# Toeplitz blocks of the later steps: tiles of 8 channel pairs, two in turn, in place of tiles of 4 pairs, four in turn

## The reference

```
y = x + depthwise_causal_conv1d(x, taps) + conv_bias     # 128 taps, of which 64 can reach a time step
h = taps (as the initial state, batch 128)
for t in 0..63:                                          # GRU
    r, z = sigmoid(y[:, t] @ W_i{r,z} + h @ W_h{r,z} + b)
    n    = tanh(y[:, t] @ W_in + b_in + r * (h @ W_hn + b_hn))
    h    = (1 - z) * n + z * h
    out[:, t] = y[:, t] + h
```

## Time and profile before

| | |
|---|---|
| median of 3 runs | 1245.08 us (1244.24 to 1248.44) |
| the profiled execution | 1242.02 us, of it the span of the trace 1240.2 us |
| PE, PEld, DVE, ACT busy | 96%, 80%, 43%, 40% of the span |
| DMA | 98.0 MB, mean 79 GB/s |
| Toeplitz tile loads | 128 of 128 KB, median 3.4 us from issue to landing |
| x unit loads | 64 of 256 KB, median 4.8 us |

### The profile page before, as it was taken

The page is one execution under the profiler, slowest core; times in us unless marked ns, Lnnn a source line. Parts: engine busy times, 40 slices in busy tenths (PEclk is TensorE's granted clock), DMA queues, the critical chain, the costliest instruction groups (busy, mean ns, idle before and its releaser), DMA issues.

```text
span 1240.2 us, 14912 instructions
## 1 busy us (share of the span) xinstructions
PE 1184.8 (96%) x5516; PEld 991.3 (80%) x5516; DVE 539.4 (43%) x807; ACT 493.2 (40%) x929; POOL 19.5 (2%) x19
## 2 busy tenths in 40 slices
PE   1599999999999999999999999999999999999997
PEld 0597788888878888888888888888888888888886
DVE  2254667666656333333333333333333333333333
ACT  1235677767765333323333323333322333332332
POOL 1040000000000000000000000000000000000000
PEclk9999999999999999999999999999999999999999
DMA  9999888888862211110011111011111001111100
GB/s 140 208 253 172 177 185 194 185 175 188 183 166 74 62 35 34 34 34 26 25 34 34 34 34 34 22 29 34 34 34 34 25 25 34 34 34 34 34 14 21
DMA packets 298482, 98.00 MB, mean 79 GB/s; under 512 B 226976, under 2 KB 292512, under 8 KB 296400
## 3 DMA queue, kind: packets, MB, share of 16 engines
q1 hardware_dynamic: 295920, 96.80, 35.5%
q10 hardware_dynamic: 2528, 0.76, 0.5%
HBM read 63.38 MB, written 34.14 MB: 79 GB/s over the span
## 4 chain that ended last, share of the span: by engine, by line
PE 90%; SPq 5%; ACT 2%; DVE 1%; issue 1%; DMA 1%; ACTq 0%; DVEq 0%
PE bank L737 81%; PE bank L759 4%; PE bank L726 3%; SPq L286 3%; PE bank L705 2%; SPq L331 1%; SPq L294 1%; ACT x_parts L522 1%; ACT tmp L532 0%; SPq L342 0%; DVE x_parts L632 0%; ACT bank L492 0%; DMA xT<-xres 0%; DMA toep_span<-tap_pad 0%; SPq L318 0%
## 5 line engine op out<-in xcount | busy, mean ns | idle before, releaser
L737 PE MATMUL bank<-w_ih_hi,xT_hi 128*128 128x512 f32 x768 | 306.7, 399 | 0.0
L737 PE MATMUL bank<-w_ih_hi,xT_lo 128*128 128x512 f32 x768 | 301.0, 392 | 0.0
L737 PE MATMUL bank<-w_ih_lo,xT_hi 128*128 128x512 f32 x768 | 300.9, 392 | 0.0
L737 PE MATMUL bank<-w_hh_hi,hT_hi 128*128 128x512 f32 x768 | 299.8, 390 | 0.0
L737 PE MATMUL bank<-w_hh_lo,hT_hi 128*128 128x512 f32 x768 | 299.7, 390 | 0.0
L737 PE MATMUL bank<-w_hh_hi,hT_lo 128*128 128x512 f32 x768 | 298.8, 389 | 0.0
L737 PEld LDWEIGHTS bank<-w_ih_hi,xT_lo 128*128 128x128 f32 x768 | 144.7, 188 | 31.5
L737 PEld LDWEIGHTS bank<-w_hh_hi,hT_lo 128*128 128x128 f32 x768 | 144.3, 188 | 30.5
L737 PEld LDWEIGHTS bank<-w_hh_hi,hT_hi 128*128 128x128 f32 x768 | 144.6, 188 | 28.1
L737 PEld LDWEIGHTS bank<-w_hh_lo,hT_hi 128*128 128x128 f32 x768 | 144.6, 188 | 27.5
L737 PEld LDWEIGHTS bank<-w_ih_hi,xT_hi 128*128 128x128 f32 x768 | 144.9, 189 | 26.9 <-ACT bank L492 0.3
(11 more groups left out here) (54 smaller groups left out, 812.8 us busy)
## 6 DMA issues: line engine op xcount, KB each, us to landing
x_unit<-in_x_dram SPq DMA_DIRECT2D x64, 256.0 KB, 4.8
toep_span<-kernel_parts SPq DMA_DIRECT2D x128, 128.0 KB, 3.4
out_dram<-outZ SPq DMA_DIRECT2D x256, 64.0 KB, 1.6
xT<-xres SPq DMA_DIRECT2D x63, 256.0 KB, 2.7
xres<-stage SPq DMA_DIRECT2D x32, 384.0 KB, 4.8
x_early<-in_x_dram SPq DMA_DIRECT2D x8, 512.0 KB, 13.2
xres<-early_result SPq DMA_DIRECT2D x32, 128.0 KB, 10.6
w_ih_raw<-in_L_cond_W_ih_dram SPq DMA_DIRECT2D x12, 256.0 KB, 7.6
```

The costliest lines, as they stand in the source:

```text
L737: mm = nc.tensor.matmul(psum[:, :], a[:, rows], b[w][:, cols], start=False, stop=stop and n == 2, skip_group_check=True)
```

## The change

The tiles of `toep_span` have T_PAIRS = 8 pairs (four banks), and there are two of them; the memory taken is the same. `load_toep(j)` fills tile j % 2 with two DMAs of 256 KB, in the same pieces of 256 bytes. Two tiles are loaded at the start. At each bank m that is a multiple of 4, SP waits until m banks are done and issues the load of tile m/4 + 1, which is first used by bank m + 4. PE waits for a tile at every fourth bank, and for the split of x at each even one as before. Matmuls, splits, evictions and stores are the same.

```
-    HL_RING, T_RING = 3, 4
+    HL_RING, T_RING, T_PAIRS = 3, 2, 8
...
-    TOEP = 2 * BLOCK * P
+    TOEP = 2 * T_PAIRS * P
...
             def load_toep(j):
-                unit, g = j * BLOCK // UNIT, j * BLOCK % UNIT
+                unit, g = j * T_PAIRS // UNIT, j * T_PAIRS % UNIT
                 for c in range(2):
                     ch = unit * 2 * UNIT + c * UNIT + g
-                    first = kernel_parts[ch:ch + BLOCK, :, 0:T]
-                    source = bass.AP(first.tensor, first.offset, [[1, T], [P, 2 * BLOCK], [1, T]])
+                    first = kernel_parts[ch:ch + T_PAIRS, :, 0:T]
+                    source = bass.AP(first.tensor, first.offset, [[1, T], [P, 2 * T_PAIRS], [1, T]])
...
-                if m % 2 == 0 and m >= 2 and m // 2 + 3 < NBLOCK:
+                if m % 4 == 0 and m >= 4 and m // 4 + 1 < PAIRS // T_PAIRS:
                     sp.wait_ge(conv_done, m)
-                    load_toep(m // 2 + 3)
+                    load_toep(m // 4 + 1)
...
                 if m % 2 == 0:
-                    j = m // 2
-                    pe.wait_ge(toep_loaded[j % T_RING], 32 * (j // T_RING + 1))
-                    pe.wait_ge(x_lo_ready, j + 1)
+                    j = m // 4
+                    if m % 4 == 0:
+                        pe.wait_ge(toep_loaded[j % T_RING], 32 * (j // T_RING + 1))
+                    pe.wait_ge(x_lo_ready, m // 2 + 1)
...
-                        at = (slot * 2 + low) * P
+                        tile, t_slot = (2 * m + pair) // T_PAIRS % T_RING, (2 * m + pair) % T_PAIRS
+                        at = (t_slot * 2 + low) * P
...
-                                              toep[j % T_RING][:, at:at + P],
+                                              toep[tile][:, at:at + P],
```

## The result

The changed kernel takes 1249.69 us in the median of 20 runs (1246.0 to 1257.3), the kernel before 1244.47 us (1239.9 to 1249.1, 20 runs). The medians lie 5.2 us apart. The ratio of the runs is 1.0054, with a 95% interval of 1.0039 to 1.0070, which is 6.7 us on 1244.5, between 4.9 and 8.7. The direction is the forecast one and the time lies just inside the lower end of its range (1249), but the forecast was +13.7 us, at least twice what was measured. The profiled execution took 1252.7 us, 10.7 us more than the profiled one of before, so this one pair of traces shows more than the medians do.

What follows compares the result with a forecast made beforehand. The prediction took late Toeplitz tiles in SP's queue to hold PE in steps 1 to 13. Waits 16.8 plus lower clock 6.8, less today's 9.9, gave +13.7 us: median 1258.8 us, range 1249 to 1272.

Steps and rivals of the forecast that it cites:

- What bounds the kernel: Steps 1 to 13: PE is held by late Toeplitz tiles in SP's program-order queue, not by DVE; 9.9 us lost.
- The deadline: Tile loads: lead falls from 6 bank intervals to 4, of 2.17 us each, 4.3 us less.
- Where the loads stand in SP's queue: Tile loads behind output stores and x quarters: SP gets 1 to 3 us ahead at best, never ahead of outZ.
- The sum: Steps 1 to 13: waits 16.8 us plus lower clock 6.8, together 23.6, less today's 9.9: +13.7 us.
- 1.8 us earlier by the freed SP time: Bank 84, step 9: load issued at 299.27 today comes 1.8 us earlier, lands at 302.1; wait 4.3 us.
- a freed 0.6 us (up to 1.4) a tile: SP's queue: two large issues replace four of 0.67 us, freeing 0.6 (up to 1.4) us for 8 pairs.
- The first rival's mechanism: SP's queue: time goes by number of issues, not bytes; 6.2 us gained, 1239 us; chance 0.08.
- The price of a pair of 256 KB: Tile load: a pair lands 4.6 us after its first issue (4.0 to 5.2); 6.3 us at bank 56.
- The places: Waits at banks 8, 24, 36, 56, 84, 104: 1.9, 0.7, 1.5, 3.3, 4.3, 4.3 us; elsewhere 0.8.
- The clock: Behind waits at banks 8, 56, 84 and 104: lower PE clock, 4 x 1.7 = 6.8 us.
- The profiled execution as a base: Whole kernel: profiled 1242.0 us becomes 1255.7; the median, 3.1 us higher at 1245.1, becomes 1258.8.
- they stay: Step 1: waits of 0.62 and 0.86 us at banks 3 and 7, which begin no tile, remain.

Runs made afterwards that it cites:

- the move of one line in SP's program: Kernel before with the tile load of point 0 issued ahead of the wait for outZ and the four output stores: 1237.99 us, ratio 0.9954.
- lead 4 alone: Kernel before, its 128 KB DMAs and tiles of 4 pairs kept, each tile asked for 4 banks ahead, not 6: 1260.13 us, ratio 1.0141.
- changed, small DMAs: Changed kernel, same tiles and schedule, each tile filled by four DMAs of 128 KB: 1263.67 us, ratio 1.0162.
- the fifth tile of 4 pairs: Kernel before with T_RING = 5, each tile of 4 pairs asked for 8 banks ahead, not 6: 1239.56 us, ratio 0.9966.
- the last version above: Changed kernel with loads of points 0 and 2 ahead of the output stores, bank 8's tile after x unit 1's second quarter: 1245.53 us, ratio 1.0019.

## Why the prediction was half right

**What bounds the kernel: right.** The waits at banks 8, 86 and 106, which the profile of before puts down to DVE, were late tiles. The changed kernel moved them from banks 86 and 106 to 84 and 104, the move of one line in SP's program took those two away but for 0.2 us, and in no trace of the changed kernel is there a tile wait at a bank with m mod 4 = 2.

**The deadline: right, and larger than the whole result.** "The lead goes from 6 bank intervals to 4": alone it costs 16.4 us.

**Where the loads stand in SP's queue: the step that failed.** The sum put the load for bank 84 "1.8 us earlier by the freed SP time" than the load behind the stores in the kernel before, and the one for bank 104 up to 3 us earlier. The row to compare with 288.67 above is the transposes of step 8 in the kernel before; the second row is step 8 of the run with four DMAs of 128 KB a tile.

```profile
283.40 0.60 PE L705 MATMUL bank<-ident,h 128*128 128x128 f32 x4
296.69 0.60 PE L707 MATMUL bank<-ident,h 128*128 128x128 f32 x4
```

The tile load behind the stores came 299.27 - 283.40 = 15.9 us after them; in the changed kernel it comes 301.15 - 288.67 = 12.5 us after, 3.4 us ahead and not 1.8. The same distance in every trace, in us from the transposes of the step before to the issue of this load, and in the last column the mean wait of the changed kernel, forecast and measured:

| load of point 0 of step | before, three traces | lead 4 alone | changed, small DMAs | changed, three traces | wait |
|---|---|---|---|---|---|
| 3 (bank 24 after) | 14.4, 16.1, 15.6 | 14.9 | 13.7 | 11.3, 12.5, 11.4 | 0.7, 2.2 |
| 9 (bank 84 after) | 15.9, 15.6, 15.8 | 12.8 | 13.1 | 12.5, 12.3, 12.2 | 4.3, 2.8 |
| 11 (bank 104 after) | 17.2, 18.3, 18.6 | 14.2 | 12.8 | 12.0, 11.6, 12.0 | 4.3, 2.4 |

So the waits at banks 84 and 104 were put 1.5 and 1.9 us too long, and these 3.4 us are nearly the whole excess of the forecast waits. The text took a freed 0.6 us (up to 1.4) a tile. Where the queue had room it was 2.62 - 1.30 = 1.3 us, near its upper end. But that is the smaller part of what moved these two loads: with small DMAs, where nothing is freed, they stand at 13.1 and 12.8 us already, and the halved issues add only about 0.7 and 1.0 us. Only in step 3 is it the larger part. The sum had no term for the rest: it carried the queue of the kernel before over, as if the other loads left it equally full. It does not stay so. Here are the first x quarter of step 8 in the kernel before and in the changed one, each behind the stretch of some 2 us ahead of it (the number before the last is the share of the DMA engines):

```profile
280.00:281.80 1.80, 1.80 (x12) 1.43 (x11) 1.53 (x3) 1.80 (x6) 0.00 (x0) 1.00 1.10 247
281.83 4.09 SPq L331 DMA_DIRECT2D x_unit<-in_x_dram  x2
284.00:286.20 2.20, 2.20 (x15) 1.94 (x14) 1.89 (x4) 2.20 (x6) 0.00 (x0) 1.00 0.00 0
286.27 1.95 SPq L331 DMA_DIRECT2D x_unit<-in_x_dram  x2
```

In the kernel before three tile loads and a store of results stand just ahead of this quarter, and in the changed kernel the engines have run dry. That PE's earlier waits also give the queue time to catch up would fit the column of the lead alone, which has the tiles and DMAs of before and still stands 3 to 4 us ahead of it in steps 9 and 11; no run separates the two.

The first rival's mechanism, time by the number of issues, which had a chance of 0.08 as an all-or-nothing case, is real and worth 14 us at this lead (1263.7 against 1249.6), but it doesn't pay for the lead. Its place was a term of the sum.

**The price of a pair of 256 KB: a little low.** 4.6 us were taken between 4.0 and 5.2; at 301.15 it was 4.9. Behind the results' stores, at bank 56, 6.3 were taken, and from the issue at 234.56 to PE's start at 242.05 it was 7.5. This worked against the error above. The median landing of a 256 KB tile DMA was 4.4 us, just over the forecast 3.7 to 4.3.

**The places.** PE's waits by the profile, in us:

| bank | forecast | the three traces |
|---|---|---|
| 8 | 1.9 | 2.9, 2.0, 2.3 |
| 24 | 0.7 | 1.9, 2.9, 1.8 |
| 36 | 1.5 | none (in the first trace tile 9 landed some 0.3 us ahead of its use) |
| 56 | 3.3 | 1.4, 1.7, 2.2 |
| 84 | 4.3 | 3.0, 2.8, 2.6 |
| 104 | 4.3 | 2.5, 2.2, 2.7 |

The forecast sum was 16.8; the three losses without low clock are about 13. That the sum came this near is in part luck: bank 24 was put 1.5 us too low and bank 36 1.5 us too high.

**The clock: right in kind, wrong as a constant.** The sum had one stretch of 1.7 us behind each of four waits (6.8 us) and two in the kernel before (3.4). The traces show five, one and three (counting the double one as two), and two, one and one. In the mean that is 5.1 against 2.3 us, +2.8 in place of +3.4. The error of this step is that one trace was read as a rule: a wait of 1.86 us was followed by low clock, one of 2.88 us at the same bank was not.

**The profiled execution as a base.** The prediction carried the 3.1 us between trace and median over unchanged. The trace of before happened to have the smallest loss of three (9.9 against a mean of 10.9), while that of the changed kernel had the largest (21.5 against 18.2). In the means: waits without clock 13 against 8.7, +4.4; clock +2.8; and -1.5 us in step 1, since the transposes of step 1 follow those of step 0 by 22.3 us in place of 23.8, which no step of the sum had. The prediction says of the waits at banks 3 and 7 that "they stay"; bank 7's did, but bank 3's (0.6, 1.1 and 1.1 us) is in none of the three traces of the changed kernel. Together these differences give +5.7, beside 5.9 in the spans and 5.2 to 6.7 in the runs. Against the +13.7: 2.2 us are the waits of the kernel before put too low, 3.7 new waits put too high, 0.6 clock, 1.5 step 1.

**Left open.** What decides whether the clock falls behind a wait of 2 to 3 us; how the 3 to 6 us that the loads behind the stores gained divide between fewer loads ahead of them and PE's own waits; why bank 3's wait went; and whether a third tile of 8 pairs would win, which no run tried (it takes twice the memory of the fifth tile of 4 pairs).

## What to carry to other kernels

Halving the number of buffers and doubling their size keeps the memory and halves the issues, but takes lead: count the lead in units of work, write out which load stands behind which in the issuing queue, and compare both prices. Before buying lead with memory, look at what a load waits behind: one load moved ahead of four stores won as much (5.8 us) as a fifth buffer (5.0 us; the intervals overlap), and took no memory. And a queue's delay in one kernel is not a constant to carry into the next: it depends on what the changed schedule puts ahead of each load. And where a waiting engine can lose its clock, take two or three traces before a wait's price is written down.

## What the runs showed of the hardware

In the six traces of the two kernels the granted clock fell to its lower level (0.50) for stretches of about 3.4 us, once for 6.8, at waits of 1.8 to 3.4 us, and stayed at 1.00 behind others of 2.9 and 2.2 us at the same places in the program. In the last version above it was low for 6.7 us at the wait of 4.61. An issue of a 256 KB DMA of 256-byte pieces took SP no longer than one of 128 KB where the queue had room (0.65 against 0.66 us each), while its landing took 4.1 in place of 3.3 us.
